# Attention of a four-stage graph network: K and V rows of 3 in 32 edge tiles from one-hot products instead of gathers

## The reference, cut to what matters

```python
Q_h = (x @ Wq + bq).reshape(N, 8, 12)
K_h = (x @ Wk + bk).reshape(N, 8, 12)
V_h = (x @ Wv + bv).reshape(N, 8, 12)
E = (edge_attr @ We + be).reshape(-1, 8, 12)
score = K_h[src] * Q_h[dst] / sqrt(12) * E
score = exp(clip(score.sum(-1, keepdims=True), -5.0, 5.0))
msg = V_h[src] * score
h_out = segment_sum(msg, dst) / (segment_sum(score, dst) + 1e-6)
x = layernorm(x + h_out)
```

## Time and profile before

| | us |
|---|---|
| median of 3 runs | 2855.43 |
| lowest, highest | 2844.96, 2857.28 |
| the profiled execution | 2861.03 |
| its span, first to last instruction | 2859.0 |
| of it the attention, from 1457 | 1402 |

### The profile page before, as it was taken

How to read it: one execution, slowest core, us unless ns; L and a number is a source line. 1 busy time by engine, 2 the same in 40 slices (tenths; PEclk the granted TensorE clock), 3 DMA queues, 4 the chain that set the end, 5 groups by cost and what they waited for, 6 DMA issues and landing times. The chain is left out here.

```text
span 2859.0 us, 49209 instructions
## 1 busy us (share of the span) xinstructions
PE 1987.2 (70%) x14740; PEld 1732.1 (61%) x14741; DVE 1414.6 (49%) x3320; ACT 1002.5 (35%) x2660; POOL 949.6 (33%) x891
## 2 busy tenths in 40 slices
PE   1888888877999999989625555555655555555556
PEld 0656565555899999967414455454555554555545
DVE  8998898984411024322423444344444444444445
ACT  2787787772200001121312233233333232333323
POOL 1122222210000000000155565555655565555652
PEclk9998898997999999999655555555555555555555
DMA  1476776686887777666244444444444444444442
GB/s 46 69 111 96 119 113 102 105 126 185 288 287 288 290 290 283 227 206 208 61 123 127 115 120 120 112 118 119 122 124 117 123 125 113 118 120 119 129 118 55
DMA packets 226599, 417.16 MB, mean 146 GB/s; under 512 B 132014, under 2 KB 151492, under 8 KB 216644
## 3 DMA queue, kind: packets, MB, share of 16 engines
q1 hardware_dynamic: 187585, 334.92, 43.0%
q0 software_dynamic: 38784, 79.48, 10.7%
HBM read 347.87 MB, written 66.43 MB: 145 GB/s over the span
## 5 line engine op out<-in xcount | busy, mean ns | idle before, releaser
L2271 POOL DMA_INDIRECT attention_windowed_vkv<-kv_dram,ttention_windowed_vsrc x808 | 788.2, 975 | 572.5 <-DVE attention_windowed_vmsg L2439 328.6
L2375 PE MATMUL attention_windowed_vps_s<-attention_windowed_hot,attention_windowed_vmsg 128*104 128x32 f32 x1616 | 320.7, 363 | 619.7 <-DVE attention_windowed_vmsg L2439 554.0
L2375 PEld LDWEIGHTS attention_windowed_vps_s<-attention_windowed_hot,attention_windowed_vmsg 128*104 128x104 f32 x1616 | 296.0, 288 | 653.8 <-DVE attention_windowed_vmsg L2439 456.7
L2363 PE MATMUL attention_windowed_vps_e<-attention_windowed_vwe,attention_windowed_vattr 97*128 97x96 f32 x1616 | 405.0, 432 | 29.8 <-issue 26.1
L654 ACT ACTIVATE add_edges_hot_lo<-add_edges_hot_lo,add_edges_parts 128x128 bf16<-128x128 bf16 x1212 | 371.2, 387 | 137.3 <-DVE add_edges_hot_lo L771 127.6
L1236 PE MATMUL graph_layers_acc<-graph_layers_w_tab,graph_layers_g 125*96 125x125 f32 x3750 | 417.7, 269 | 0.0
L1236 PEld LDWEIGHTS graph_layers_acc<-graph_layers_w_tab,graph_layers_g 125*96 125x96 f32 x3750 | 406.6, 163 | 0.0
L2363 PEld LDWEIGHTS attention_windowed_vps_e<-attention_windowed_vwe,attention_windowed_vattr 97*128 97x128 f32 x1616 | 367.0, 332 | 33.2 <-issue 27.3
L2304 ACT ACTIVATE attention_windowed_vmsg<-ttention_windowed_vscore 128x32 f32<-128x32 f32 x202 | 46.3, 229 | 912.3 <-DVE ttention_windowed_vscore L2435 581.2
L702 PE MATMUL add_edges_ps_four<-add_edges_hot,add_edges_hot_lo 128*128 128x200 bf16 x2424 | 351.2, 268 | 0.0
L2429 DVE TENSOR_TENSOR attention_windowed_vprod<-attention_windowed_vkv,attention_windowed_vps_q 128x384 f32<-128x384 f32 x202 | 111.2, 551 | 367.6 <-remote 299.1
(11 more groups left out here) (233 smaller groups left out, 2508.4 us busy)
## 6 DMA issues: line engine op xcount, KB each, us to landing
graph_layers_w_tab<-w_blocks SPq DMA_DIRECT2D x75, 1562.5 KB
graph_layers_c_tab<-c_blocks SPq DMA_DIRECT2D x75, 800.0 KB
w_blocks<-add_edges_strip SPq DMA_DIRECT2D x25, 1562.5 KB, 16.9
attention_windowed_vattr<-in_attr_T SPq DMA_DIRECT2D x202, 192.0 KB
attention_windowed_vdrow<-dstf_dram SPq DMA_DIRECT2D x202, 192.0 KB
c_blocks<-add_edges_counts SPq DMA_DIRECT2D x25, 800.0 KB, 15.1
attention_windowed_vkv<-kv_dram,ttention_windowed_vsrc POOLq DMA_INDIRECT x808
ttention_windowed_q_rows<-q_dram SPq DMA_DIRECT2D x202, 18.0 KB
```

The source lines that it names most:

```text
L2271: nc.gpsimd.indirect_dma_start(out=kv[s][:, k, :], out_offset=None, in_=kv_dram, in_offset=bass.IndirectOffsetOnAxis(ap=src4[s][:, k:k + 1 ...
L2363: nc.tensor.matmul(ps_e[s % 2][:, k, :], attr[:, s, k * P:(k + 1) * P], wes[:], start=True, stop=True)
L2375: last = nc.tensor.matmul(ps_s[s % 2][:], msg[s][:, k, :], hot[s][:, k, :], start=k == 0, stop=k == Q4 - 1)
```

## The change

Of the 32 tiles of a round the last tiles of slots 1, 3 and 6 (`OWN`) are no longer gathered, from round 2 on (slot 1 from round 3 on). POOL's `gather` issues 3 instead of 4 transfers there. PE makes the rows instead. The table of all 3125 nodes stands in SBUF in 25 chunks of 125 nodes, each float32 value split in three bfloat16 parts that add up to it; a one-hot tile of 125 nodes x 128 edges for each chunk, as weights, times the 192 columns of each part, all 75 summed in one PSUM bank, gives the 128 rows. That is 225 matmuls a round, in the 8 slots 36, 39, 24, 24, 27, 24, 24, 27 (`CHUNKS_IN_SLOT` times 3). ACT copies each finished tile from PSUM into `kv` (`take_own`).

The one-hots need, for each edge, its source's lane (0 to 124) and chunk (1 to 25): the **codes**. POOL makes them for all edges at the start of `graph_layers` and writes them to `code_dram`. In the attention SP loads those of a round with six transfers, each 128 values sent to 125 partitions (`load_codes`), behind the loads of slot 2. DVE makes `tile_at` out of them (L2638) in slot 1 and then 25 one-hots (L2642), in the slots 0, 3, 4, 4, 4, 4, 3, 3 of them (`HOTS_IN_SLOT`), always for the round after. In rounds 0 and 1 SP loads the table in five pieces, and ACT and DVE split it, ten instructions of 125 x 960 elements on each.

`ps_s` has one buffer instead of two, the PSUM bank of `ps_o` is now shared with the first own tile, and the normalised result is written over `x`, so that one `store` buffer falls away. DVE's and SP's loops have one round in a body.

```diff
+OWN = (1, 3, 6)
+OWN_FROM = 2
@@ attention_windowed, SP
+            def load_codes(i):
+                if reaches(i, OWN_FROM + 1):
+                    sp.wait_ge(tile_at_ready, i - OWN_FROM)
+                first = (SLOTS * Q4 * P) * i + (Q4 * OWN[1] + Q4 - 1) * P
+                step = Q4 * (OWN[2] - OWN[1]) * P
+                for k in range(2):
+                    for u in range(OWNS):
+                        sp.dma_start(codes[0:L, k, u, :], code_dram[k, bass.ds(first + u * step, P)].partition_broadcast(L)).then_inc(codes_landed, 16)
+            def load_round(i):
                 for s in range(SLOTS):
                     load(i, s)
+                    if s == 2 and reaches(i, OWN_FROM):
+                        load_codes(i)
@@ POOL
-                for k in range(Q4):
+                for k in range(Q4 - by_own(i, s)):
@@ ACT
+            def take_own(i, u):
+                group = SLOTS * i + OWN[u + 1] if u + 1 < OWNS else SLOTS * (i + 1) + OWN[0]
+                slot = OWN[(u + 1) % OWNS]
+                act.wait_ge(own_ps, own_count(i, u))
+                act.wait_ge(msg_ready, group - SLOTS + 1)
+                nc.scalar.copy(kv[slot][:, Q4 - 1, :], ps_own[u][:, 0:2 * D]).then_inc(own_ready, 1)
+                    weigh(i, s)
+                    if s == 0 and reaches(i, OWN_FROM + 1):
+                        take_own(i - 1, 2)
+                    if s == 2 and reaches(i, OWN_FROM):
+                        take_own(i, 0)
+                    if s == 5 and reaches(i, OWN_FROM):
+                        take_own(i, 1)
@@ PE
+            def own_rows(i, par, s):
+                begin = sum(CHUNKS_IN_SLOT[:s])
+                for n in range(begin, begin + CHUNKS_IN_SLOT[s]):
+                    u, t = divmod(n, NT)
...
+                    for part in range(3):
+                        done = nc.tensor.matmul(ps_own[u][:, 0:2 * D], own_hot[0:L, par, t, u, :], table[0:L, t, part * 2 * D:(part + 1) * 2 * D],
+                                                start=t == 0 and part == 0, stop=t == NT - 1 and part == 2)
@@ DVE
+            def own_hots(i, s):
+                n = i - OWN_FROM
+                if s == 1:
+                    if reaches(n, 2):
+                        dve.wait_ge(own_ps, OWNS * n - OWNS)
...
+                    dve.wait_ge(codes_landed, 96 * (n + 1))
...
+                    nc.vector.scalar_tensor_tensor(tile_at[0:L], codes[0:L, 0], lane[0:L], codes[0:L, 1], ALU.is_equal, ALU.mult).then_inc(tile_at_ready, 1)
+                    dve.wait_ge(tile_at_ready, n + 1)
+                begin = sum(HOTS_IN_SLOT[:s])
+                for t in range(begin, begin + HOTS_IN_SLOT[s]):
+                    done = nc.vector.tensor_scalar(own_hot[0:L, par_of(i), t, :, :].squeeze(1), tile_at[0:L], float(t + 1), None, ALU.is_equal)
...
                     attend(i, s)
                     prepare(*later(i, s, 2))
+                    if HOTS_IN_SLOT[s] and reaches(i, OWN_FROM - 1) and not (isinstance(i, int) and i == ROUNDS - 1):
+                        own_hots(i + 1, s)
                     add(*later(i, s, -1))
                     weigh(i, s)
```

253 lines of the change are left out of this document (178 added, 75 removed).

## The result

The changed kernel takes 3098.31 us (median of 4 runs, 3081.83 to 3111.68), the kernel before beside it 2856.36 us (2844.96 to 2871.91). The ratio is 1.0847, 95% interval 1.0798 to 1.0897: slower, by 242 us where 130 were forecast. The execution that was profiled took 3081.83 us, its span is 3079.9.

What follows compares the result with a forecast made beforehand. Waits bound the attention: PE's signals are held while POOL issues gathers. Terms -87 + 98 + 72 + 36 + 12 = +131 gave 2992 us on the profiled execution, 2986 on the median, stated as 2985; range 2805 to 3115.

Steps and rivals of the forecast that it cites:

- The sign: Whole kernel: the change makes it slower, chance 0.74, against 0.21 for faster and 0.05 for within 0.5%.
- codes wait: DVE's slot 1 waits 7.0 us for SP's six transfers, plus 0.55 for the instruction, 3.3 regained: +98 us, bounds 0 and 210.
- gathers: POOL in the attention: 69 gathers less, each worth its 1.26 us of issuing about once: -87 us, bounds 0 and 118.
- one-hots and own products: DVE's 575 one-hots at 0.30 us, 42% counting: +72; PE's 225 matmuls a round, slower at half clock: +36.
- my own loop: Attention: signals arrive, DVE makes one message, POOL starts the gathers it frees, PE's next signals are held until those end.
- The favourable case: DVE's slot 1 was itself started by a held signal that SP got too, so it waits 5.3 us, not 8.6.
- the 3.3 us to be given back: One DVE idle time each round, regained because PE's products for slot 2 arrive while DVE waits for the codes.
- the upper bound: POOL's gathers in the attention: if everything scales with them, 69 fewer save 118 us.
- PE at 1.2 GHz throughout: Rival: PE stays at the lower clock and bounds the attention, 12.8 us in 23 rounds, +294, 3161 us; chance 0.10.
- The gathers slowed by the one-hots: Rival: each of DVE's 575 one-hots stops POOL for 0.30 us, gathers longer by 128 us, 3113 us; chance 0.07.
- The gathers as the whole story: Rival: codes and one-hots fit DVE's idle time, PE runs at 2.4 GHz: 2786 us, up to 2845; chance 0.22.
- The start: Rounds 0 and 1: ten DVE instructions of 960 float32 elements splitting the table, +12 us, bounds 0 and 24.

Runs made afterwards that it cites:

- kind A: Chips, not a change: those on which the unchanged kernel before takes about 2856 us, 54.4 us a round of the attention; the result was measured on one.
- the stages of one kernel: Changed kernel with successive attention stages: as is 63.2 us a round, codes early 54.6, also 1 one-hot of 25 54.6, also a third of own products 52.5.
- kind B: Chips, not a change: those on which the unchanged kernel before takes about 2510 us, 40.6 us a round of the attention.
- the experiment on the bytes: Kernel before, each gather fetching 96 of a row's 192 floats from round 1 on: 2509.40 us against 2508.37, ratio 1.0010.

## Why the prediction came out as it did

The sign, and that the codes wait is the largest new cost, were right; so was the reason, that what stands between a signal and the message counts. The sum was 112 us too low: 242 us were measured against 130. By its steps, on kind A, with the 22 full rounds:

| step | forecast, us | by the runs, us |
|---|---|---|
| gathers | -87 | 22 x (49.0 - 54.4) = -119 |
| one-hots and own products | +72 + 36 = 108 | 22 x (54.6 - 49.0) = +123 |
| codes wait | +98 | 22 x (64.7 - 54.6) = +222 |
| sum of these | +119 | +226 |

The result itself is +242. The stages behind the last column have five or six rounds each, but for the 54.4 and 64.7. By the spread of their rounds each term is uncertain by some 30 to 60 us (an estimate), some of them were taken on different chips of kind A, and the rest is within that.

*Codes.* This term was mis-sized by 124 us, or by 91 if the codes wait is taken as 8.6 us a round from the stages of one kernel: about the whole miss. Two steps of it failed. The first is PE's part: I had its sums, products and Q rows, 3.8 us behind the message, and left out that the own products of slot 0, 36 matmuls that I had counted myself, stand ahead of those sums. With the signal's delay the part is 7.1 us, 3.3 more. On kind B the same products stand there and the part is only 3.3 us, since they are done earlier: their place alone is not the cost. What makes them late on kind A, PE's stops, the late signals or the clock, no run separates. The second is a choice between two ends. I had worked out a wait of 8.6 us and of 5.3 in case the signal had been held anyway, and took 7.0. But by my own loop the message of slot 0 starts a run of four gathers, and PE's next signal, the very one that SP needs, ends inside it. The favourable case needed the opposite and was not open. Held or not, the wait is 11.7 us on kind A and 8.4 on kind B. And of the 3.3 us to be given back 1.6 to 3.1 came: 11.7 us of waiting cost 8.6 to 10.1 a round, with the 2 us of uncertainty.

*Gathers.* On kind A they gave 5.4 us a round, uncertain by 1.5, so rather more than "its 1.26 us at most about once" (3.8); the upper bound, everything scaling with them, fits better, and the stage can't exclude the forecast. On kind B the term is right to 4 and 10 us (83 and 77), since POOL does nothing else there.

*One-hots and own products.* Together 15 us off, which is luck, since one by one they were wrong: the one-hots cost nothing that shows on kind A (54.6 and 54.6) where I had 72 us, though one takes 0.28 us, close to the 0.30 of the forecast; and the own products, the copies and what they delay cost the whole 123 where I had 36. Their term had only the clock's price, 2.3 us in a fifth of the slots. What it lacked, as far as the traces show, is PE's stops. PE's idle time that ends in "issue", in which it waits for nothing that the profile shows, is 10.7 us a round in the stage with the codes early, 2.0 in the stage with 29 gathers and no own products, and 3.4 with a third of them. Not all of it is on the path: two thirds of the own products less took 7.3 us a round off these stops and 2.1 off the round, while the granted clock fell from 0.84 to 0.54, so the two effects aren't told apart. The other 3.5 us are not taken apart either. Two of PE's waits from 1757 to 2957 us in the trace of the result (us, times, longest), and then its own products on kind B, of which the last number is all the idle time ahead of them:

```profile
PE attention_windowed_vps_e L2471 <- issue: 87.3, 128, 1.9
...
PE tention_windowed_vps_own L2513 <- issue: 31.3, 43, 1.2
```
```profile
L2526 PE MATMUL tention_windowed_vps_own<-attention_windowed_table,tention_windowed_own_hot 125*128 125x192 bf16 x905 | 88.1, 260 | 0.0
```

The 119.3 us ahead of L2591 I had not looked for. The turned sums stand behind 24 own products of slot 5, but that is the smaller part: 91 of the 119.3 us lie behind the end of the transposition, like the other waits that "remote" ends. On kind B DVE waits there 1.7 us in each round, behind the same products.

*The rivals.* PE at 1.2 GHz throughout: no, the clock is 0.77 and PE is busy 73% of the stage; it goes up and down, as expected. The gathers slowed by the one-hots: 955 ns here, no; on kind B only with the one-hots behind the message (1.33 us beside them against 0.96). The gathers as the whole story: no, though on kind B with the codes early it is nearly so (-55 of -83 us). The codes on DVE's slot 1 did not find idle time to hide in on either kind.

*The start.* Nothing of its 12 us is seen: the first gather of round 3 follows 146 us behind the first of round 0, against 150 before, with two gathers less between them.

## What to carry to other kernels

When a transfer is put into a queue, follow what its queue waits for back to the message that starts it, and count everything that stands ahead on each engine, the change's own new work first. Load what is needed once a round a full round ahead: here this one place is worth 9 to 10 us a round on one kind of chip and 9 on the other, more than the 5.4 and 3.7 that three gathers less save, and it turns 8.6% slower into about the same on the one, and some 6% slower (by the estimate above) into 2% faster on the other. With that version a round takes 37.9 us against 40.6 on kind B (the kernel as a whole 2457 against 2512), and 54.6 against 54.4 on kind A, where it wasn't run as a whole.

## What was not expected of the hardware

Two kinds of chips, 2856 and 2510 us for one and the same kernel, with the attention at 54.4 or 40.6 us a round. On the first, SP's load follows 1.2 to 1.5 us behind POOL's last gather in 18 of 22 rounds, and DVE waits over a third of the time for "remote"; on the second the load follows 0.23 us behind PE's products in each of the six rounds of that stage, in five of them while a gather is being issued. What makes them differ, and whether it is the issuing or the transfers that hold the signals, stays open: the experiment on the bytes met a chip without the effect. It may not be the signals alone that are late: on the first kind PE also stops within groups of matmuls that wait for nothing, beside gathers and shortly behind them, which it does neither on the second kind nor in the kernel before. So a wait that "remote" ends may be one for a late signal or one of an engine that is itself held, and no run tells them apart. A third thing: the effect is gone on the first kind too once the gathers are 16 a round, 33.3 and 33.1 us.
